# Norm factors on Pool instead of ACT and DVE, later xT transposes, and output-weight casts placed further back in the queues

## The chip, the cores and the metric

The kernel runs on one Trainium2 chip, on 8 cores, each with one of the 8 batch elements; the cores don't exchange data. A core has TensorE (PE), VectorE (DVE), ScalarE (ACT), GpSimd (Pool), and SyncE (SP), which issues most of the loads. The metric is device time in microseconds of the slowest core.

## What is computed

T = 2048 rows of D = 1024 per core. After a first layer norm, the block adds the state-space branch (with a layer norm of its own) and a feed-forward branch with ternary weights:

```python
xn = _layernorm(x, axis=-1)
x = x + _L0_attn_ref(xn, ...) + _L0_ffn_ref(xn, ...)

# _L0_attn_ref(x, ...): residual = x, second layer norm, then
dA = jnp.exp(-jnp.exp(log_A) * dt[:, None]); dB = B_param * dt[:, None]
h = dA * h + dB * u[..., None]                        # scan over time
y = jnp.einsum('dn,bdn->bd', C_param, h) + D_param * u
return residual + jnp.einsum('btd,ed->bte', y, W_out) + b_out

# _L0_ffn_ref(x, ...):
scale = jnp.maximum(jnp.mean(jnp.abs(w)), 1e-08)
w_t = jnp.clip(jnp.round(w / scale), -1.0, 1.0)       # W1 and W2
h = jax.nn.gelu(jnp.einsum('bsd,fd->bsf', x, w_t1) + b1, approximate=False)
return jnp.einsum('bsf,df->bsd', h, w_t2) + b2
```

## The kernel before

The program has one hand-written instruction order for each engine, with semaphores between them; no scheduler moves anything. What stands in a queue runs in that order.

**Stage 1, the state-space branch**, goes over 16 chunks c of 128 rows. For each chunk: `load_x` brings x into one of four buffers `gx`; DVE takes mean and variance (`stats`, `aggregate`, for groups of one chunk up to chunk 3 and of two chunks from chunk 4); the inverse root of the variance `rstd` and the shift `sb` give the normalised `xn` (`normalise`, on ACT, for chunk 0 on DVE); the second norm needs one more factor, `rstd2`, which scales the tables PP and cQ (`scale_PP` on ACT for chunks 1 to 3, `scale_tables` on DVE). DVE makes five products u = xn * gm (`make_u`, L854) and the running state S with its operand V (`make_V`, L870 and L874). PE then runs, for each chunk, `chunk_Q` (L1010, the chunk's part of the state), `ssm_local` (L1037, 40 matmuls into pY, within the chunk), `ssm_state` (L1044, what comes from earlier chunks), `transpose_V` (L1020), `transpose_x` (L1001, xn into the layout xT that stage 2 needs) and `wout` (L1061, 16 matmuls of 512 columns with the output weights). ACT evicts each: `yT_evict`, `VT_evict`, `xT_evict`, `yW_evict`; the last goes to memory through a Pool DMA (`store_yw`). The output weights come as four fp32 blocks (`load_wo` on SP) and are cast to bf16, two on ACT, two on DVE (`cast_wo`, L525 and L777); `wout(0)` waits for all four.

**The inverse roots before.** For a group, ACT takes the square root of the variance (`sqrt1`, L531), DVE the reciprocal, sb, and the second norm's variance y2 (`finish1`, L757 to L767), ACT its root (`sqrt2`, L537), DVE the reciprocal (`finish2`, L772). So each group passes from DVE to ACT and back twice. The constant EAGER = 12 shifts these, `normalise`, `wout` and the transposes between two orders, one for early chunks and one for late ones.

**At the start** PE and DVE also make six moments from the parameters (`power`, `moment`, L1080 and L1084, `moment_columns`, L1094), which `state_factors` on DVE (L827 to L835) turns into the factors that the state's operands need. `keep_clock` are matmuls without use.

**Beside stage 1** ACT sums |W1| over 16 blocks (`abs1`), which SP streams through buffers in the order W1_ORDER. After the last sum DVE sets the threshold and begins to quantise W1 (`quant`). **Stage 2** is the feed-forward part on PE: `mm1` (L1191, 4 x 32 tiles), then `mm2` (L1210); the last `wout(15)` stands ahead of it in PE's queue.

Pool's queue holds the x loads from chunk 4 on (each waits for the `normalise` that frees the buffer) and the `store_yw`s.

Of the kernel before, what the change touches and what calls it, by code (L numbers as in the profile page):

```python
# [45 lines left out]
EAGER = 12  # L46
# [52 lines left out]
def build_nc():  # L99
# [122 lines left out]
    sd = small("sd", M)  # L222
# [3 lines left out]
    sd2 = small("sd2", M)  # L226
# [40 lines left out]
    with st:  # L267
# [43 lines left out]
        s_sq1 = sem("s_sq1")  # L311
# [3 lines left out]
        s_sq2 = sem("s_sq2")  # L315
# [25 lines left out]
        with nc.Block() as blk:  # L341
            @blk.sync
            def _(sy):
# [36 lines left out]
                load_wo(0)  # L380
                load_wo(1)
                load_wo(2)
                load_x(2)
# [83 lines left out]
            def _(gp):  # L467
                gp.memset(Va[0][:, :], 0.0)
# [5 lines left out]
                gp.dma_start(wv[1][RW:RW + NV, :], cWE_in.ap()).then_inc(d_we, 16)  # L474
                def load_x(c):
# [19 lines left out]
                store_yw(3)  # L495
                for i in range(4, M):
                    if i + 7 < M:
                        load_x(i + 7)
                    store_yw(i)

            @blk.scalar
            def _(ac):
# [11 lines left out]
                ac.activation(dump[:, 1:2], cst[:, 0:1], AF.Sqrt, bias=cst[:, 2:3])  # L514
                mv3 = mv.ap().rearrange("p (c two) -> p c two", two=2)
# [11 lines left out]

                def sqrt1(g):
                    cs = slice(GROUPS[g][0], GROUPS[g][-1] + 1)
                    ac.wait_ge(s_var, g + 1)  # L530
                    ac.activation(sd.ap().unsqueeze(2)[:, cs, :], mv3[:, cs, 1:2], AF.Sqrt,  # L531
                                  bias=cst[:, 2:3]).then_inc(s_sq1, 1)

                def sqrt2(g):
                    cs = slice(GROUPS[g][0], GROUPS[g][-1] + 1)
                    ac.wait_ge(s_rs, g + 1)
                    ac.activation(sd2[:, cs], y2[:, cs], AF.Sqrt,  # L537
                                  bias=cst[:, 2:3]).then_inc(s_sq2, 1)
# [67 lines left out]
                gm_evict(0)  # L606
                sqrt1(0)
                gm_evict(1)
# [664 lines left out]
```

## Time and profile before

| | |
|---|---|
| times of 3 runs | 608.58, 610.12, 629.5 us (median 610.12) |
| profiled execution | 607.71 us, span of the slowest core 606.1 us (cores 600.9 to 606.1) |
| PE busy | 579.3 us, 96% |
| PE weight loads busy | 296.4 us, 49% |
| DVE busy | 271.5 us, 45% |
| ACT busy | 239.4 us, 40% |
| Pool busy | 21.6 us, 4% |
| read / written | 88.95 / 16.78 MB |

The profile is of one execution, on the core that was slowest. Busy time counts what an engine executes; overlapping matmuls are pipelined, so PE's share is not its share of peak. In the rows below "[x <-A y Lz]" means that the engine was idle for x us before the instruction and that the end of y on engine A (line z) released it.

### The profile page before, as it was taken

What the parts mean: (1) busy time and instruction counts of PE and PEld (TensorE: products, weight loads), DVE (VectorE), ACT (ScalarE), POOL (GpSimd) and SP (SyncE); (2) the same over time, 40 slices, a digit from 0 to 9 for tenths busy, and PEclk for the clock granted to TensorE, in tenths of its full rate; (3) what the DMA queues carried; (4) which work ended last, traced back from release to release, by engine and by line L of the source; (5) the groups of instructions that cost most, each with busy time, mean ns of one, the idle gap of its engine ahead of it and who ended that gap; (6) DMA issues with size and microseconds to landing.
All of it is one profiled execution on the core that took longest, in us unless ns stands there. A gap on an engine that the chain in (4) does not pass through costs nothing.

```text
span 606.1 us, 9213 instructions; the slowest of 8 cores (600.9 to 606.1 us)
## 1 busy us (share of the span) xinstructions
PE 579.3 (96%) x3478; PEld 296.4 (49%) x3478; DVE 271.5 (45%) x461; ACT 239.4 (40%) x310; POOL 21.6 (4%) x38
## 2 busy tenths in 40 slices
PE   7679799899999999999999999999999999999998
PEld 2456566567444444444444444444444444444445
DVE  6586978765699700000098861022332222222232
ACT  3677898788644577777344433100000000000000
POOL 3001111000100000000000000000000000000000
PEclk9779999899999999999999999999999999999999
DMA  6996768839778355571109952022333332232221
GB/s 161 325 335 256 252 213 317 301 124 356 247 269 278 151 202 198 201 258 47 45 31 304 317 197 83 1 105 104 111 134 135 135 113 104 105 105 104 105 104 70
DMA packets 21855, 106.10 MB, mean 175 GB/s; under 512 B 2922, under 2 KB 3434, under 8 KB 14388
## 3 DMA queue, kind: packets, MB, share of 16 engines
q1 hardware_dynamic: 17284, 90.50, 43.2%
q0 software_dynamic: 4128, 14.91, 7.0%
q8 instruction: 29, 0.48, 0.4%
q14 instruction: 14, 0.11, 0.1%
q10 hardware_dynamic: 400, 0.10, 0.1%
HBM read 88.95 MB, written 16.78 MB: 174 GB/s over the span
## 4 chain that ended last, share of the span: by engine, by line
PE 81%; DVE 6%; DMA 4%; ACT 3%; issue 3%; DVEq 2%; SPq 1%; ACTq 0%
PE pQ L1210 10%; PE pQ L1191 9%; PE pY L1210 9%; PE pX L1191 9%; PE pW L1210 9%; PE pW L1191 9%; PE pY L1191 9%; PE pX L1210 9%; PE pW L1061 5%; DMA wos<-wo 3%; DVE u L854 2%; PE pY L1037 2%; DVE bns L741 1%; DMA lBC_s<-abc 1%; DVEq L751 1%
## 5 line engine op out<-in xcount | busy, mean ns | idle before, releaser
L1210 PE MATMUL pQ<-w2q,h 128*128 128x512 fp8e4 (+1 forms) x288 | 59.6, 367 | 0.0
L1191 PE MATMUL pQ<-xT,w1q 128*128 128x512 bf16 x256 | 57.9, 379 | 0.6 <-DVE w1q L931 0.6
L1191 PE MATMUL pY<-xT,w1q 128*128 128x512 bf16 x256 | 57.9, 379 | 0.0
L1191 PE MATMUL pX<-xT,w1q 128*128 128x512 bf16 x256 | 57.9, 379 | 0.0
L1191 PE MATMUL pW<-xT,w1q 128*128 128x512 bf16 x256 | 57.9, 379 | 0.0
L1061 PE MATMUL pW<-woT,yT 128*128 128x512 bf16 x240 | 55.2, 383 | 1.8 <-ACT yws L603 1.8
L1210 PE MATMUL pY<-w2q,h 128*128 128x512 fp8e4 x256 | 55.9, 379 | 0.0
L1210 PE MATMUL pW<-w2q,h 128*128 128x512 fp8e4 x256 | 55.9, 379 | 0.0
L1210 PE MATMUL pX<-w2q,h 128*128 128x512 fp8e4 (+1 forms) x256 | 52.5, 366 | 0.0
L854 DVE TENSOR_TENSOR u<-xn,gm 128x1024 bf16<-128x1024 bf16 x80 | 49.5, 683 | 0.3 <-ACT gm L520 0.2
L1210 PEld LDWEIGHTS pQ<-w2q,h 128*128 128x128 bf16 x288 | 28.2, 98 | 30.5
L1191 PEld LDWEIGHTS pQ<-xT,w1q 128*128 128x128 fp8e4 x256 | 25.0, 98 | 31.0 <-issue 1.1
L1210 PEld LDWEIGHTS pY<-w2q,h 128*128 128x128 bf16 x256 | 25.1, 98 | 30.2
L1191 PEld LDWEIGHTS pX<-xT,w1q 128*128 128x128 fp8e4 x256 | 25.1, 98 | 30.2
L1191 PEld LDWEIGHTS pW<-xT,w1q 128*128 128x128 fp8e4 x256 | 25.0, 98 | 30.2
L1191 PEld LDWEIGHTS pY<-xT,w1q 128*128 128x128 fp8e4 x256 | 25.0, 98 | 30.2
L1210 PEld LDWEIGHTS pW<-w2q,h 128*128 128x128 bf16 x256 | 24.9, 97 | 30.3
L1037 PE MATMUL pY<-PP,u 128*128 128x128 bf16 x600 | 37.9, 224 | 0.7 <-ACT yT L596 0.7
L1210 PEld LDWEIGHTS pX<-w2q,h 128*128 128x128 bf16 x256 | 25.1, 98 | 27.0
L1061 PEld LDWEIGHTS pW<-woT,yT 128*128 128x128 bf16 x240 | 23.1, 99 | 27.5 <-issue 3.2
L1037 PEld LDWEIGHTS pY<-PP,u 128*128 128x128 bf16 x600 | 35.5, 101 | 1.3 <-issue 0.7
L950 DVE TENSOR_REDUCE tot<-ab 128x1 f32<-128x16 f32 x1 | 0.2, 171 | 76.5 <-ACT junk L707 76.5
(145 smaller groups left out, 610.9 us busy)
## 6 DMA issues: line engine op xcount, KB each, us to landing
kr<-w SPq DMA_DIRECT2D x20, 1024.0 KB, 6.2
p<-w SPq DMA_DIRECT2D x13, 1024.0 KB, 7.1
g<-w SPq DMA_DIRECT2D x9, 1024.0 KB, 9.3
scr_yw<-yws POOLq DMA_DIRECT2D x16, 512.0 KB, 7.0
xr<-x SPq DMA_DIRECT2D x16, 512.0 KB, 4.7
yr<-scr_yw SPq DMA_DIRECT2D x16, 512.0 KB, 5.5
out<-osb SPq DMA_DIRECT2D x15, 512.0 KB, 3.0
gx<-x POOLq DMA_DIRECT2D x12, 512.0 KB, 8.1
```

Of the source, the lines that this page charges most:

```text
L741: dv.bn_stats(bns[:, c * 12 + 6:c * 12 + 12], gx[c % 4][:, 512:1024])
L751: dv.drain()
L854: return dv.tensor_tensor(u[c % 2][k][:, :], xn[c % 4][:, :], gm[k][:, :], ALU.mult)
L950: dv.tensor_reduce(tot[:, 1:2], ab2[:, :], AX.X, ALU.add).then_inc(s_tot2, 1)
L1037: te.matmul(pS[c][:, bs], u[c % 2][k][:, bs], PP[c % 2][:, k * 128:(k + 1) * 128], start=(n == 0 and b % 4 == 0), stop=False)
L1061: inst = te.matmul(pO[i][:, hf * 512:(hf + 1) * 512], yT[i % 2][:, b * 128:(b + 1) * 128], woT[:, q:q + 512], start=(b == 0), stop=(b == 7))
L1191: inst = te.matmul(pA[n % 8], w1q8[:, f * 1024 + k * 128:f * 1024 + (k + 1) * 128], x3[:, k, :, :], start=(k == 0), stop=(k == 7))
L1210: inst = te.matmul(out_psum(e, n, cs), h[b][:, f * BT + tk * 128:f * BT + (tk + 1) * 128], w2q8[:, f * 1024 + cs.start:f * 1024 + cs.stop] ...
```

## The change

1. `finish` on Pool makes everything that `sqrt1`, `finish1`, `sqrt2` and `finish2` made: the variance plus EPS to the power -0.5 with Pool's pow, sb, sa, and the same for the second norm. Nine small operations for a group, with drains between those that depend on each other. ACT has no square root any more (and no table for it), DVE no reciprocal.
2. `transpose_x(c + 2)` and `xT_evict(c + 2)` in the loop over the chunks become (c + 1), behind `transpose_V` and `VT_evict`. The constant EAGER goes: one order for all chunks from 4 on, in which `wout(c - 1)` ends the chunk on PE and `normalise(c + 2)` ends it on ACT.
3. DVE's two weight casts stand behind `make_V(2)` (before: one ahead of `state_factors`, one behind `make_V(1)`), ACT's first one behind `scale_PP(1)`. x(2) is loaded ahead of the second weight block; its statistics stand ahead of `state_factors`.
4. `moment(4)` runs behind `transpose_x(0)`, with eight `keep_clock` matmuls in its old place; `keep_clock` writes pQ instead of pX.

```diff
-EAGER = 12
@@ SP
                 load_x(1)
                 load_wo(0)
+                load_x(2)
                 load_wo(1)
                 load_wo(2)
-                load_x(2)
                 load_wo(3)
@@ Pool
+                def finish(g):
+                    gp.wait_ge(s_var, g + 1)
...
+                    n = len(GROUPS[g])
+                    gp.tensor_scalar(v1, var, EPS, None, ALU.add)
+                    gp.drain()
+                    gp.tensor_tensor(rstd[:, cs], vt1[:, cs], nhalf[:, 0:n], ALU.pow)
+                    gp.drain()
+                    gp.tensor_tensor(sb.ap().unsqueeze(2)[:, cs, :], mean, r, ALU.mult)
+                    gp.tensor_tensor(v1, var, r, ALU.mult)
+                    gp.drain()
+                    gp.tensor_scalar(sb[:, cs], sb[:, cs], -1.0, None, ALU.mult)
+                    gp.drain().then_inc(s_rs, 1)
+                    gp.tensor_tensor(y2[:, cs], vt1[:, cs], rstd[:, cs], ALU.mult)
+                    gp.tensor_scalar(sa[:, cs], rstd[:, cs], 1.0, None, ALU.add)
+                    gp.drain()
+                    gp.tensor_scalar(y2[:, cs], y2[:, cs], EPS, None, ALU.add)
+                    gp.drain()
+                    gp.tensor_tensor(rstd2[:, cs], y2[:, cs], nhalf[:, 0:n], ALU.pow)
+                    gp.drain().then_inc(s_rs2, 1)
+
+                finish(0)
+                finish(1)
                 load_x(4)
                 load_x(5)
+                finish(2)
                 load_x(6)
                 store_yw(0)
+                finish(3)
                 load_x(7)
                 store_yw(1)
+                finish(4)
                 load_x(8)
                 store_yw(2)
                 load_x(9)
+                store_yw(3)
+                finish(GROUP_OF[6])
                 load_x(10)
...
+                for c in range(5, M + 1):
+                    store_yw(c - 1)
+                    if c + 6 < M:
+                        load_x(c + 6)
+                    if c % 2 == 1 and c + 3 < M:
+                        finish(GROUP_OF[c + 3])
@@ ACT, the loop after
+                for c in range(4, M):
                     yT_evict(c)
                     if c + 1 < M:
                         VT_evict(c + 1)
+                        xT_evict(c + 1)
+                    if c == 4:
+                        abs1(2)
+                    if c < M - 1:
+                        abs1(c - 1)
+                    if c >= M - 2:
+                        abs1(c)
+                    yW_evict(c - 1)
+                    if c + 2 < M:
+                        normalise(c + 2)
@@ DVE
                 stats_group(1)
-                finish1(1)
-                cast_wo(2)
+                stats(2)
                 state_factors()
                 make_u(1)
                 make_V(1)
+                dv.drain()
+                aggregate(2)
+                make_V(2)
+                cast_wo(2)
                 cast_wo(3)
-                stats_group(2)
-                make_V(2)
-                finish1(2)
+                make_u(2)
                 stats_group(3)
...
@@ PE
                 bc_pair(pB[4], 3)
-                moment(4)
+                keep_clock(8)
                 ssm_local(0)
...
                 transpose_x(0)
+                moment(4)
                 moment(5)
...
+                for c in range(4, M):
                     if c + 1 < M:
                         chunk_Q(c)
                     ssm_local(c)
                     ssm_state(c)
-                    if c + 3 < EAGER:
-                        wout(c - 1)
-                    if c + 2 < M:
-                        transpose_x(c + 2)
                     if c + 1 < M:
                         transpose_V(c + 1)
-                    if EAGER <= c + 3:
-                        wout(c - 1)
+                        transpose_x(c + 1)
+                    wout(c - 1)
```

**DVE's queue between the statistics of chunk 1 and its products.** Before (out<-in: what is written, then what is read; woT are the cast output weights, wos the fp32 blocks, Va and mst what `state_factors` writes, rstd_155 the second norm's factor):

```order
L745 BN_AGGR mv<-bns 128x2
L757 RECIPROCAL rstd<-sd 128x1 [waits s_sq1]
L759 TENSOR_TENSOR vt_152<-mv,rstd 128x1
L761 SCALAR_TENSOR_TENSOR sb<-mv,rstd 128x1
L765 TENSOR_TENSOR y_153<-vt_152,rstd 128x1
L767 TENSOR_SCALAR sa<-rstd 128x1
L777 CAST woT<-wos_59 128x2048 [waits d_wo2]
L827 TENSOR_TENSOR Va_99<-pQ,pars 128x8x6 [waits s_mom,d_par,s_zero]
```

The same place after:

```order
L727 BN_AGGR mv<-bns 128x2
L722 BN_STATS bns<-gx_107 128x6 [waits d_x2]
L723 BN_STATS bns<-gx_107 128x6
L787 TENSOR_TENSOR Va_99<-pQ,pars 128x8x6 [waits s_mom,d_par,s_zero]
L791 TENSOR_TENSOR Va_99<-pars 128x8
L787 TENSOR_TENSOR Va_100<-pQ,pars 128x8x6
```

The factors of chunk 1's norm and the cast, with its wait for the third weight block, are no longer ahead of `state_factors`; the statistics of chunk 2 are.

**Pool's queue around chunks 4 to 7, after** (before, only its DMA rows stood there; `scr_yw<-yws` is a `store_yw`, `gx<-x` a `load_x`, the rows between are one `finish`, here that of chunks 6 and 7):

```order
L501 DMA gx_106<-x 128x1024 [waits s_xn]
L506 DMA scr_yw<-yws_110 128x1024 [waits s_yWev]
L482 TENSOR_SCALAR vt_151<-mv 128x2 [waits s_var]
L484 TENSOR_TENSOR rstd<-vt_151,nhalf 128x2
L486 TENSOR_TENSOR sb<-mv,rstd 128x2
L487 TENSOR_TENSOR vt_151<-mv,rstd 128x2
L489 TENSOR_SCALAR sb<-sb 128x2
L491 TENSOR_TENSOR y_152<-vt_151,rstd 128x2
L492 TENSOR_SCALAR sa<-rstd 128x2
L494 TENSOR_SCALAR y_152<-y_152 128x2
L496 TENSOR_TENSOR rstd_154<-y_152,nhalf 128x2
L501 DMA gx_107<-x 128x1024 [waits s_xn]
```

The nine operations stand behind a store that waits for ACT's `yW_evict(3)`, and a load of x stands behind them.

**ACT's queue around `normalise(6)`.** Before (rw and res are blocks of W1 for `abs1`; xn_87 is the buffer of chunk 6):

```order
L531 ACTIVATE sd<-mv,cst 128x2 [waits s_var]
L596 ACTIVATE yT_89<-pY 128x1024 [waits s_ssm,s_wout]
L545 ACTIVATE xn_87<-gx_107,sb,rstd 128x1024 [waits s_rs,s_Q,s_u]
L537 ACTIVATE sd_154<-y_153,cst 128x2 [waits s_rs]
L589 ACTIVATE rwA,ab_159<-rwA 128x2048 [waits d_rw0]
L603 ACTIVATE yws_110<-pW 128x1024 [waits s_wout,d_yw1]
```

After:

```order
L614 ACTIVATE yT_89<-pY 128x1024 [waits s_ssm,s_wout]
L589 ACTIVATE VTs_98<-pQ 128x512 [waits s_vtr,s_ssm]
L582 ACTIVATE xT<-pX 128x1024 [waits s_T]
L607 ACTIVATE rwA,ab_158<-rwA 128x2048 [waits d_rw0]
L607 ACTIVATE junk,ab_158<-res_0_50 128x2048 [waits d_res1_0,s_ab1]
L621 ACTIVATE yws_110<-pW 128x1024 [waits s_wout,d_yw1]
L563 ACTIVATE xn_87<-gx_107,sb,rstd 128x1024 [waits s_rs,s_Q,s_u]
L614 ACTIVATE yT_90<-pY 128x1024 [waits s_ssm,s_wout]
```

`normalise(6)` came right behind yT(4); it now comes behind two |W1| sums and yW(3), and the square roots are gone.

## Rows read from the trace of the kernel before

**Rows 1.** By stage: window, length; busy PE, PEld, DVE, ACT, POOL; clock; DMA share, GB/s.
```profile
33.20:62.40 29.20, 24.36 (x275) 17.95 (x273) 21.44 (x59) 22.63 (x30) 2.79 (x5) 0.94 0.78 277
62.40:114.50 52.10, 45.59 (x519) 32.09 (x516) 40.71 (x105) 45.93 (x57) 6.91 (x13) 0.97 0.83 286
114.50:143.80 29.30, 28.19 (x343) 20.48 (x340) 20.63 (x49) 24.61 (x28) 2.13 (x4) 1.00 0.58 194
...
161.10:606.10 445.00, 442.26 (x2080) 203.43 (x2080) 160.00 (x164) 118.25 (x162) 1.25 (x1) 1.00 0.41 144
```
**Rows 2.** Timeline (start, length, instruction): `ssm_local` of chunks 1, 3, 4, 6, 10.
```profile
33.22 4.04 PE L1037 MATMUL pY<-PP,u 128*128 128x128 bf16 x40
...
53.64 2.39 PE L1037 MATMUL pY<-PP,u 128*128 128x128 bf16 x40 [0.68 <-ACT yT L596]
...
62.41 2.68 PE L1037 MATMUL pY<-PP,u 128*128 128x128 bf16 x40
...
80.07 2.39 PE L1037 MATMUL pY<-PP,u 128*128 128x128 bf16 x40
...
114.48 2.39 PE L1037 MATMUL pY<-PP,u 128*128 128x128 bf16 x40
```
**Rows 3.** Timeline, PE: a `wout`, then `ssm_local` of chunks 12 and 13.
```profile
126.12 3.61 PE L1061 MATMUL pW<-woT,yT 128*128 128x512 bf16 x16
...
129.77 2.39 PE L1037 MATMUL pY<-PP,u 128*128 128x128 bf16 x40
...
136.78 2.39 PE L1037 MATMUL pY<-PP,u 128*128 128x128 bf16 x40
```
**Rows 4.** Timeline: moments on PE, casts and `state_factors` on DVE.
```profile
23.73 1.07 PE L1084 MATMUL pQ<-wk,cCs 128*64 128x512 f32 x2
...
25.97 1.03 PE L1094 MATMUL pQ<-cEs,mrow 64*128 64x12 f32 x8 [1.17 <-ACT mrow L619]
...
29.67 1.23 DVE L777 CAST woT<-wos 128x2048 bf16<-128x2048 f32 x1 [3.70 <-DMA wos<-wo]
30.82 0.22 DVE L827 TENSOR_TENSOR Va<-pQ,pars 128x48 bf16<-128x48 f32 x1
...
35.83 1.22 DVE L777 CAST woT<-wos 128x2048 bf16<-128x2048 f32 x1
```
**Rows 5.** Timeline: chunk 0 from its variance to xn and PP.
```profile
14.32 0.21 DVE L745 BATCH_NORM_AGGREGATE mv<-bns 128x2 f32<-128x12 f32 x1
...
16.28 0.81 DVE L812 TENSOR_SCALAR xn<-gx,rstd,sb 128x1024 bf16<-128x1024 f32 x1
...
18.25 0.55 DVE L848 TENSOR_SCALAR PP<-PF,rstd 128x640 bf16<-128x640 f32 x1 [0.23 <-issue]
```
**Rows 6.** Timeline, Pool: a one-column memset and a DMA issue.
```profile
0.49 0.10 POOL L100 MEMSET const-float32-0.0<- 128x1 f32 x1 [0.49 <-issue]
...
46.02 0.54 POOL L482 DMA_DIRECT2D scr_yw<-yws  x1 [2.44 <-ACT yws L603]
```
**Rows 7.** Timeline, ACT: one late chunk.
```profile
132.76 1.02 ACT L596 ACTIVATE yT<-pY 128x1024 bf16<-128x1024 f32 x1 [1.63 <-PE pY L1044]
...
133.69 1.02 ACT L564 ACTIVATE xT<-pX 128x1024 bf16<-128x1024 bf16 x1
...
134.59 0.60 ACT L571 ACTIVATE VTs<-pQ 128x512 bf16<-128x512 bf16 x1
...
135.07 1.25 ACT L545 ACTIVATE xn<-gx,sb,rstd 128x1024 bf16<-128x1024 f32 x1
136.20 1.92 ACT L589 ACTIVATE junk<-kr 128x2048 bf16<-128x2048 f32 x1
...
138.09 1.03 ACT L603 ACTIVATE yws<-pW 128x1024 f32<-128x1024 f32 x1
```
**Rows 8.** Waits: who waited for whom, us in total, times, longest.
```profile
DVE rstd L757 <- ACT sd L531: 12.1, 8, 3.4
```
**Rows 9.** Timeline, PE: the first matmuls of the feed-forward part.
```profile
161.12 3.61 PE L1191 MATMUL pQ<-xT,w1q 128*128 128x512 bf16 x16 [0.59 <-DVE w1q L931]
```

More of the change, by code:

```diff
@@ L225, in build_nc @@
     y2 = small("y2", M)
-    sd2 = small("sd2", M)
+    nhalf = small("nhalf", 2)
     rstd2 = small("rstd2", M)
@@ L467, in _ @@
             def _(gp):
+                gp.memset(nhalf[:, :], -0.5)
                 gp.memset(Va[0][:, :], 0.0)
@@ L809, in _ @@
                 power(4)
-                finish1(0)
-                dv.drain()
+                dv.wait_ge(s_rs, 1)
                 dv.tensor_scalar(xn[0][:, :], gx[0][:, :], rstd[:, 0:1], sb[:, 0:1],
@@ L841, in scale_tables @@
                 def scale_tables(c):
-                    if c == GROUPS[GROUP_OF[c]][0]:
-                        finish2(GROUP_OF[c])
+                    dv.wait_ge(s_rs2, GROUP_OF[c] + 1)
                     if c == 0:
@@ L900, in _ @@
                 stats_group(4)
-                finish1(4)
                 for c in range(3, M):
-                    if c % 2 == 0 and c + 2 < EAGER:
-                        finish1(GROUP_OF[c + 2])
-                    if c % 2 == 1 and EAGER <= c + 3 < M:
-                        finish1(GROUP_OF[c + 3])
                     if c + 1 < M:
@@ L909, in _ @@
                         make_u(c + 1)
-                    if c % 2 == 1 and c + 3 < EAGER:
+                    if c == 4:
+                        stats_group(GROUP_OF[6])
+                    if c >= 5 and c % 2 == 1 and c + 3 < M:
                         stats_group(GROUP_OF[c + 3])
-                    if c % 2 == 0 and EAGER <= c + 4 < M:
-                        stats_group(GROUP_OF[c + 4])
                 def set_threshold(src, o):
@@ L1099, in keep_clock @@
                     for _ in range(n):
[L1100 removed]
+                        te.matmul(pQ[:, 0:128], Va[0][:, 0:128], Va[0][:, 0:128],
                                   start=True, stop=True)
@@ L1133, in _ @@
                 ssm_state(1)
-                wout(0)
                 transpose_V(2)
                 transpose_x(2)
+                wout(0)
+                chunk_Q(2)
                 wout(1)
-                chunk_Q(2)
                 ssm_local(2)
                 ssm_state(2)
+                transpose_V(3)
                 transpose_x(3)
-                transpose_V(3)
                 chunk_Q(3)
@@ L1146, in _ @@
                 wout(2)
+                transpose_V(4)
                 transpose_x(4)
-                transpose_V(4)
-                chunk_Q(4)
-                ssm_local(4)
-                ssm_state(4)
-                wout(3)
-                transpose_x(5)
-                transpose_x(6)
-                transpose_V(5)
-                for c in range(5, M):
+                for c in range(4, M):
                     if c + 1 < M:
```

113 lines of the change are left out of this document (15 added, 98 removed).

## The prediction, as put on record before the run

> **What bounds the kernel now.** I read the table by stage first [rows 1]. From 161.1 us to the end (the two products of the feed-forward part) PE is busy 442.3 of 445.0 us at a granted clock of 1.00, and no edit touches an instruction there. What can move is the stage ahead of it: when the first L1191 matmul starts, 161.12 us [rows 9]. In that stage the same table shows PE busy 28.2 of 29.3 us late (chunks 10 to 13), but only 24.4 of 29.2 and 45.6 of 52.1 us in the two stretches before: 4.8 and 6.5 us of idle.
>
> The starts of `ssm_local` turn this into a pace [rows 2, 3]. From chunk 12 to chunk 13 a chunk takes 136.78 - 129.77 = 7.0 us, full of PE work; its longest piece, `wout`, is half of it (3.61 us, some 3.5 from its start to the next piece's). From chunk 4 (62.41) to chunk 10 (114.48) six chunks take 52.07 us, 8.7 each, where six at the late pace would take 42.0. Both stretches hold six `wout`s, so 10 us are lost there. Chunk 1 starts at 33.22 and chunk 3 at 53.64.
>
> The waits name two causes. DVE waits 12.1 us in eight pieces for ACT's small square roots [rows 8], in order, with its tables, products and state updates queued behind. And at 29.67 DVE's queue had stood 3.70 us for the third output weight to land, with `state_factors` behind that cast, so at 30.82 [rows 4]. Its input, the moment columns, was done at 25.97 + 1.03 = 27.0.
>
> **The change part by part.** Times are of the profiled execution: span 606.1 us, 607.71 us by the clock of the runs, against a median of 610.12 over three runs of which the lowest is 608.58. I take 607.7.
>
> 1. **Casts moved, x(2) loaded earlier.** DVE's wait for the weight goes. `state_factors` then waits for the moments, which come later: `moment(4)` now runs behind `ssm_local(0)`, so the columns end one warm fp32 product (1.07 us, [rows 4]) later, 28.1. Gain 30.8 - 28.1 = 2.7 us. The eight `keep_clock` matmuls put in its old place lie in a gap in which PE waits for PP of chunk 0; I cost them at nothing, and without that cover at under 1 us. What is late next is `wout(0)`, which needs all four casts: the fourth weight is used by DVE at 35.83 before, the cast takes 1.2 us (as in [rows 4]), so 37.0, while PE reaches `wout(0)` at 37.3 through ACT's queue. That leaves 2.6 us of gain.
>
> 2. **Inverse roots on Pool.** Per group 9 small operations on one or two columns, 5 of them (with four drains) before s_rs, 4 before s_rs2. Before, the same for chunk 0 ran from the variance (14.32 + 0.21) to xn at 16.28, and to PP at 18.25 [rows 5]: 1.75 and 3.7 us. No Pool arithmetic is in the trace. Nearest rows below: a one-column memset, 0.10 us; nine make 0.9 us. Above: a Pool DMA issue, 0.54 us [rows 6]; nine make 4.9 us. A drained step needs read, write and drain, and pow is more than an add, so I take 0.39 us a step: P1 = 2.0 to s_rs, P2 = 1.5 more to s_rs2. For chunk 0 that is 3.5 against 3.7 us, so no gain or loss at the start. From DVE it removes the 12.1 us of waits and seven small operations a group; from ACT 18 square roots of 0.3 us and a table load.
>
> 3. **Pool's queue.** Pool also issues the x loads and the yW stores, in order. `finish(3)` stands behind `store_yw(0)` and `finish(5)` behind `store_yw(3)`; each issue waits for ACT's eviction and takes 0.54 us [rows 6]. I walked the queues with the durations of [rows 7] (yT and xT 0.9, VT 0.5, xn 1.1, abs 1.9, yW 1.0 us from start to start).
>  Chunk 3: its variance is there at about 41.9; the store is issued by 42.5; s_rs2 at 42.5 + 3.5 = 46.0; then on ACT PP 0.8, yW(1) 1.0, abs 1.9 + 0.2, yT(2) 0.9: `ssm_local(3)` at 50.8 instead of 53.64, gain 2.8.
>  Chunk 4: state of chunk 3 at 53.8, `wout(2)` 3.5, transposes and chunk_Q 1.2: 58.4 instead of 62.41, gain 4.0. Chunk 5 follows at the full pace, 65.4.
>  Chunk 6: ACT ends xn(5) at 61.4, then yT 0.9, VT 0.5, xT 0.9, two abs 3.8 and yW(3) 1.0: 68.6. The store 0.5, P1 2.0, xn(6) 1.2: 72.4, where PE wanted it at 68.7. Transpose 0.5, `wout(4)` 3.5 and chunk_Q 0.3 follow: 76.7 instead of 80.07, gain 3.4.
>
> 4. **Transposes one chunk later, no EAGER switch.** From chunk 6 on nothing is late: ACT needs 0.9 + 0.5 + 0.9 + 1.9 + 1.0 + 1.1 = 6.4 us per chunk, DVE 20.63 of 29.3 us [rows 1] less what is removed, Pool's results are due 5 us after they come. So 7.0 us a chunk: chunk 10 at 104.7 instead of 114.48, gain 9.8. One more hitch goes: chunks 10 to 12 took 129.77 - 114.48 = 15.3 us where two at the late pace take 14.0, so 11.1 from chunk 12 on. At the end ACT is the queue that decides when the last |W1| sum is ready; it now has xT(15) in the last stretch, 0.9 us [rows 7]. Gain 10.2 us.
>
> Sum: 2.7 - 0.1 (wout(0)) + 0.2 (chunk 3) + 1.2 (chunk 4) - 0.6 (chunk 6) + 6.4 (to chunk 10) + 1.3 - 0.9 = 10.2. 607.7 - 10.2 = **597.5 us**.
>
> The Pool price enters three times: chunk 0 once P1 + P2 passes 3.7, chunk 3 with P1 + P2, chunk 6 with P1. With 0.9 us in all chunk 3 is held by yW(1) instead (1.2 us better) and chunk 6 is 1.5 better: gain 12.9, 594.8 us. With 4.9 us: 1.2 + 1.4 + 0.7 lost, gain 6.9, 600.8 us.
>
> **The rivals.**
> - *DVE and Pool stand in each other's way.* [rows 1] speaks against much of it: late DVE is busy 70%. For it: Pool's nine steps fall into the same stretch as the five products. If each Pool step waits out half a product (0.3 us) and stops DVE for 0.2 us, P1 + P2 becomes 6.2 us: that costs chunk 0 2.5, chunk 3 2.7 and chunk 6 1.4 us less what lies beside idle DVE time (most of chunk 0), some 5 us. Gain about 5: 602.7 us. The Trainium skill, page "SBUF — State Buffer", section "Who interferes with whom", says that a DVE instruction with two SBUF inputs and a Pool instruction that reads SBUF exclude each other for a whole instruction; no row here shows it, since Pool reads nothing before.
> - *Pool is slow the first time.* A first arithmetic operation on Pool that costs several microseconds would hold xn(0), and everything behind. With 6 us (taken as eleven of Pool's 0.54 us issues) less 0.2 of slack: gain 4.4, 603.3 us. The Trainium skill's "GPSIMD Engine Reference", section 2.1, gives approximately 6 us for the first call of a freshly loaded kernel; whether the plain operations count as that the page doesn't say. No row shows such a gap ahead of Pool's first memset.
> - *Slower than before: the Pool chain itself.* If a drained Pool step with pow costs 0.9 us, P1 = 4.5 and P2 = 3.6. Chunk 0 loses 8.1 - 3.7 = 4.4, chunk 3 8.1 - 3.5 = 4.6, chunk 6 4.5 - 2.0 = 2.5 us against my sum: 11.5, so 609.0 us. The point from which it decides, where 23 steps less 9.2 eat the 10.2, is a step of 0.84 us. Against it: no Pool row of small size exceeds 0.54 us.
> - *The gain is given back to loads.* The stage needs the same bytes in 10 us less. DMA share is 0.83 in the middle and 0.58 late [rows 1], so there is room; the x loads are issued later on Pool, and if one lands 1 us late in each of three groups, it costs 3 us: 600.5 us. Inside my range.
>
> **How the numbers follow.** My forecast (gain 6.9 to 12.9) has 0.60, the collision 0.15, the first-time cost or a chain of 0.6 to 0.8 us a step 0.15, slower than before 0.07, and 0.03 for a gain over 13. The likeliest one's own range is 594.8 to 600.8. Leaving out no more than 2 in 10 I give 592.5 to 606.0, which takes in the collision and the slow first call. Two per cent is about what a measurement of this kernel tells from no change: 12.2 us, so below about 596. That needs a step under some 0.2 us or a smoother walk than mine: 0.30. Within 2%: 0.65. Slower by over 2% needs a step of well over a microsecond: 0.05.
>
> **What would show it.** In the profile after: s_var to xn(0) about 2.0 us and to PP(0) 3.5 us, the small Pool rows 0.1 to 0.5 us; `state_factors` at 28.1 with no wait for a weight; chunk 3 near 50.8, chunk 4 near 58.4, PE waiting about 3.5 us for xn(6) behind `store_yw(3)`, chunk 6 near 76.7; chunks 7 to 14 each 7.0 us; the first L1191 matmul (other line number) at 151 us, and 445 us from there. I am wrong if the late pace isn't 7.0, if Pool's steps cost 0.6 us or more, or if DVE's products get longer than 0.68 us beside Pool's work. A granted clock that is low for longer around 20 to 28 us would delay the moments by up to 1 us.

## The result, and the profile after

The changed kernel takes 645.98 us (median of four runs, 644.96 to 647.02). The ratio to the kernel before is 1.060, 95% interval 1.056 to 1.064: 6% slower, where 597.5 us and a gain were forecast. (The runs of before beside it are 608.58 and 610.12 us; two more, 627.84 and 629.5, show a lower clock on one die, and such runs are left out of every ratio here, though not of the medians.) In the profiled execution the slowest core, 7, has a span of 645.4 us, the others 632.0 and more.

The page of the changed kernel first: busy time, then the granted clock in 40 slices of 16 us.

```profile
span 645.4 us, 9264 instructions; the slowest of 8 cores (632.0 to 645.4 us)
## 1 busy us (share of the span) xinstructions
PE 586.7 (91%) x3486; PEld 300.6 (47%) x3486; DVE 264.7 (41%) x401; ACT 234.6 (36%) x288; POOL 51.5 (8%) x129
...
PEclk9779778998799999999999999999999999999999
```

The digit is 7 or 8 in seven of the first 11 slices and 9 in all later ones. The table by stage (window, length; busy PE, PEld, DVE, ACT, POOL; clock; DMA share, GB/s) answers to [rows 1]:

```profile
30.70:57.30 26.60, 15.42 (x121) 9.93 (x122) 11.29 (x22) 10.76 (x12) 3.97 (x12) 0.75 0.73 249
...
65.70:138.60 72.90, 54.59 (x587) 39.18 (x588) 39.00 (x86) 47.14 (x52) 19.17 (x49) 0.87 0.68 202
138.60:146.40 7.80, 7.17 (x90) 5.12 (x87) 6.62 (x15) 6.57 (x7) 1.45 (x3) 1.00 0.96 346
164.70:182.20 17.50, 9.49 (x91) 5.99 (x88) 4.37 (x9) 6.71 (x9) 3.25 (x9) 0.71 0.56 198
200.00:645.00 445.00, 442.27 (x2080) 203.45 (x2080) 160.52 (x165) 118.75 (x162) 1.25 (x1) 1.00 0.42 144
```

The feed-forward part is what it was: 442.27 busy of 445.00 us at full clock. All the loss lies ahead of it. It begins at 200.43 us instead of 161.12 [rows 9]. The rows show the pattern that begins with chunk 4: one chunk of each pair takes 7 to 8 us (138.6 to 146.4, chunk 10), the other 8.8 to 21 (164.7 to 182.2, chunk 13, with no engine busy for more than 9.5 of its 17.5 us).

The waits say for whom (engine, line, for whom; us in total, times, longest):

```profile
POOL rstd L484 <- issue: 50.5, 9, 12.2
ACT xn L563 <- POOLq L490: 41.9, 7, 11.0
DVE PP L807 <- POOLq L497: 38.4, 6, 12.6
PE pX L954 <- ACT xn L563: 36.7, 8, 11.8
```

Read from below: PE waits 36.7 us for xn, ACT makes xn late because it waits 41.9 us for the end of Pool's first half, and inside Pool's chain 50.5 us stand ahead of one instruction, the first pow (L484), "issue": the profile shows nothing that it waits for. (Of the nine pieces one, of chunk 0, is 0.33 us; eight make 50.1.) In the code there is one thing between L482 and L484: a drain.

Pool's timeline shows the same chain twice, for the groups of chunk 1 and of chunk 2 (start, length, instruction, idle before):

```profile
25.14 0.22 POOL L482 TENSOR_SCALAR vt<-mv 128x1 f32<-128x1 f32 x1 [6.35 <-DVE mv L727]
25.51 0.57 POOL L484 TENSOR_TENSOR rstd<-vt,nhalf 128x1 f32<-128x1 f32 x1
...
29.27 1.23 POOL L501 DMA_DIRECT2D gx<-x  x2 [0.70 <-ACT xn L563]
34.10 0.22 POOL L482 TENSOR_SCALAR vt<-mv 128x1 f32<-128x1 f32 x1 [3.60 <-DVE mv L727]
43.03 0.57 POOL L484 TENSOR_TENSOR rstd<-vt,nhalf 128x1 f32<-128x1 f32 x1 [8.71 <-issue]
...
159.38 0.53 POOL L506 DMA_DIRECT2D scr_yw<-yws  x1 [6.14 <-ACT yws L621]
159.94 0.24 POOL L482 TENSOR_SCALAR vt<-mv 128x2 f32<-128x2 f32 x1
172.41 0.72 POOL L484 TENSOR_TENSOR rstd<-vt,nhalf 128x2 f32<-128x2 f32 x1 [12.23 <-issue]
```

For chunk 1 the step over the drain takes 25.51 - 25.14 = 0.37 us, as I had costed it (0.39). For chunk 2, with two x loads issued at 29.27 to 30.5, it takes 8.9 us. The last group, behind the store of 159.38, takes 12.5. The DMA view gives, from issue to landing, of the stores issued at 54.28 and at 159.38:

```profile
scr_yw<-yws POOLq DMA_DIRECT2D x1, 512.0 KB, 3.1
...
scr_yw<-yws POOLq DMA_DIRECT2D x1, 512.0 KB, 12.8
```

54.28 + 3.1 = 57.4, and that group's pow starts at 57.58; 159.38 + 12.8 = 172.2, pow at 172.41. The load issued at 107.09 (5.3 us) has landed by 112.4, pow at 112.66; that of 122.92 (8.0 us) by 130.9, pow at 131.19. In all eight groups behind the first load the pow starts 0.2 to 0.3 us after the last landing; the two groups ahead of it have gaps of 0.33 us and none. The other seven cores show the same: over all eight there are 59 gaps of 0.9 us and more, and each ends 0.2 to 0.43 us after the last landing of a transfer that Pool had issued. That is the theory: **a drain on Pool waits until the transfers that Pool issued have landed**, though here nobody needs them.

The end of the chain, on PE, in the last pair:

```profile
164.68 2.39 PE L990 MATMUL pY<-PP,u 128*128 128x128 bf16 x40
...
175.75 1.01 PE L954 MATMUL pX<-cIDb,xn 128*128 128x128 bf16 x8 [8.01 <-ACT xn L563]
176.56 5.58 PE L1014 MATMUL pW<-woT,yT 128*128 128x512 bf16 x16
...
185.53 3.62 PE L1014 MATMUL pW<-woT,yT 128*128 128x512 bf16 x16
```

After 8.01 us of waiting the next `wout` takes 5.58 us, the following one 3.62: over 164.7 to 182.2 the granted clock is 0.71, parts of it at 1.2 GHz, parts at 2.4. Here the wait cost PE 2 us beyond its own length.

### The profile page after: what moved, and what is told of

It reads as the page before. It is cut to its first block, busy times and chain, and to the rows that moved or that the text cites. A ratio compares the mean times of both kernels' runs of the same rounds, so it can differ in the third digit from the quotient of the medians.

```text
span 645.4 us, 9264 instructions; the slowest of 8 cores (632.0 to 645.4 us)
## 1 busy us (share of the span) xinstructions
PE 586.7 (91%) x3486; PEld 300.6 (47%) x3486; DVE 264.7 (41%) x401; ACT 234.6 (36%) x288; POOL 51.5 (8%) x129
## 4 chain that ended last, share of the span: by engine, by line
PE 79%; issue 11%; ACT 5%; POOLq 2%; DVE 1%; POOL 1%; DVEq 0%; DMA 0%; ACTq 0%
PE pQ L1153 9%; PE pQ L1134 9%; PE pY L1134 9%; PE pW L1153 9%; PE pY L1153 9%; PE pX L1134 9%; PE pW L1134 9%; PE pX L1153 8%; PE pW L1014 5%; ACT xn L563 2%; PE pY L990 1%; PE pX L954 1%; POOLq L485 1%; ACT yws L621 1%; PE pQ L1033 1%
## 5 line engine op out<-in xcount | busy, mean ns | idle before, releaser
L1014 PE MATMUL pW<-woT,yT 128*128 128x512 bf16 x240 | 61.4, 414 | 1.9 <-ACT yws L621 1.9
L954 PE MATMUL pX<-cIDb,xn 128*128 128x128 bf16 x128 | 10.9, 235 | 36.7 <-ACT xn L563 36.7
L990 PE MATMUL pY<-PP,u 128*128 128x128 bf16 x600 | 39.6, 229 | 3.9 <-ACT yT L614 3.5
L1153 PEld LDWEIGHTS pQ<-w2q,h 128*128 128x128 bf16 x288 | 28.2, 98 | 30.5
L1014 PEld LDWEIGHTS pW<-woT,yT 128*128 128x128 bf16 x240 | 24.9, 106 | 32.1 <-issue 11.3
L990 PEld LDWEIGHTS pY<-PP,u 128*128 128x128 bf16 x600 | 37.2, 103 | 4.8 <-issue 4.1
```

What stands on the lines that cost most here:

```text
L954: inst = te.transpose(xbank[c % 2][:, b * 128:(b + 1) * 128], xn[c % 4][:, b * 128:(b + 1) * 128], cID[:, :])
L990: te.matmul(pS[c][:, bs], u[c % 2][k][:, bs], PP[c % 2][:, k * 128:(k + 1) * 128], start=(n == 0 and b % 4 == 0), stop=False)
L1014: inst = te.matmul(pO[i][:, hf * 512:(hf + 1) * 512], yT[i % 2][:, b * 128:(b + 1) * 128], woT[:, q:q + 512], start=(b == 0), stop=(b == 7))
L1153: inst = te.matmul(out_psum(e, n, cs), h[b][:, f * BT + tk * 128:f * BT + (tk + 1) * 128], w2q8[:, f * 1024 + cs.start:f * 1024 + cs.stop] ...
```

## The experiments

The rivals: the pow itself is slow in those places, or DVE and Pool stand in each other's way (both then independent of transfers), or the new order, not the roots, makes the gaps.

**Semaphores for the drains.** In `finish` each of the seven drains (the expectation says eight) goes. Five become a semaphore, raised by the operations ahead and waited for by Pool; behind the two that raised s_rs and s_rs2 the last operation now raises them itself:

```diff
-                    gp.tensor_scalar(v1, var, EPS, None, ALU.add)
-                    gp.drain()
+                    step(gp.tensor_scalar(v1, var, EPS, None, ALU.add))
+                    settled()                    # gp.wait_ge(s_fin, count)
```

> The changed kernel with each of Pool's eight drains per group replaced by a wait on a semaphore that the operation itself raises; order and DMAs as in the changed kernel. Theory D (a drain on Pool also waits until the DMAs that Pool issued before it have landed: the gaps of 8.7, 2.5, 7.8, 4.5, 7.3, 6.2 and 12.2 us ahead of the first pow of a group end 0.2 us after a landing): those gaps fall to 0.2 to 0.4 us, the first matmul of the feed-forward part starts at 150 to 153 us instead of 200, time 597 to 600 us. Theory Q (Pool completes nothing behind an own DMA until that has landed, drain or not): gaps and time stay, 640 to 648 us. Theory P (Pool is kept off SBUF by DVE's operations with two SBUF inputs): gaps stay where DVE is busy, 625 to 648 us.

Measured: 608.15 us, ratio to before 0.997 (0.994 to 1.000). Pool's timeline:

```profile
130.96 0.53 POOL L516 DMA_DIRECT2D scr_yw<-yws  x1 [6.44 <-ACT yws L631]
131.52 0.37 POOL L492 TENSOR_SCALAR vt<-mv 128x2 f32<-128x2 f32 x1
132.04 0.87 POOL L494 TENSOR_TENSOR rstd<-vt,nhalf 128x2 f32<-128x2 f32 x1
```

The store of 130.96 takes 11.8 us to land, and the pow (now L494) starts 1.1 us after the issue. No gap stands ahead of this pow on any core, and the 38 us are gone with nothing else changed. The gaps went as theory D had it; the time is 8 us above its 597 to 600. The section on the prediction takes up why. The times of this version fall into two groups, four runs of 603.7 to 605.0 us and five of 608.0 to 610.9. In the profiled run seven cores have spans of 600.1 to 602.8 us and one, core 5, has 606.7: rows of this run are of that core unless another is named.

**Drains kept, transfers issued by ACT.** The x loads and the yW stores move from Pool's queue to ACT's:

```diff
-                def load_x(c):                   # on Pool
-                    gp.wait_ge(s_xn, c - 3)
-                    gp.dma_start(gx[c % 4][:, :],
+                def load_x(c):                   # on ACT, store_yw too
+                    ac.wait_ge(s_xn, c - 3)
+                    ac.dma_start(gx[c % 4][:, :],
```

> The changed kernel with all drains kept, but the x loads from chunk 4 on and the stores of yW issued by ACT instead of Pool, each one operation behind the one it depends on. Pool then has only arithmetic. Theory D and theory Q: no gap over 0.4 us ahead of pow; ACT pays 28 DMA issues with short waits, so 597 to 606 us. Theory P: the gaps stay, because DVE does the same work; 625 to 648 us.

Measured: 608.26 us, 0.999 (0.997 to 1.000). Pool's timeline in chunk 2, drains in place:

```profile
35.64 0.22 POOL L482 TENSOR_SCALAR vt<-mv 128x1 f32<-128x1 f32 x1 [6.62 <-DVE mv L718]
36.00 0.57 POOL L484 TENSOR_TENSOR rstd<-vt,nhalf 128x1 f32<-128x1 f32 x1
36.71 0.19 POOL L486 TENSOR_TENSOR sb<-mv,rstd 128x1 f32<-128x1 f32 x1
36.85 1.17 POOL L487 TENSOR_TENSOR vt<-mv,rstd 128x1 f32<-128x1 f32 x1
```

0.36 us from the first operation to the pow, and 0.36 to 0.38 in every later group of this run. A drain alone costs next to nothing, and so does a transfer alone; it takes both on Pool. One thing more changed with the issuer: the profile lists the transfers under "q0 software_dynamic" in the changed kernel and under "q10 hardware_dynamic" here, so the run doesn't tell whether Pool's own issue or that kind of queue is what a drain waits for. The time, like that of the first version, is above the 597 to 606 us of theory D.

**Pairs of probes in the kernel before.** Pool makes two additions on a scratch column with a drain between them behind `store_yw` 5, 9 and 13, and with a semaphore between them behind `store_yw` 7, 11 and 14:

```diff
+                def probe_drain():
+                    gp.tensor_scalar(pr[:, 2:3], pr[:, 0:1], 1.0, None, ALU.add)
+                    gp.drain()
+                    gp.tensor_scalar(pr[:, 4:5], pr[:, 2:3], 1.0, None, ALU.add)
```

> The kernel before with probes on Pool that nobody waits for: two one-column additions with a drain between them (once with no DMA of Pool in flight, and behind the stores of chunks 5, 9 and 13) and two with a semaphore wait between them (once at the start, and behind the stores of chunks 7, 11 and 14). Theory D: from the first to the second addition 0.3 to 0.5 us with no DMA in flight; behind a store the drain pair is 3 to 12 us apart and ends 0.2 us after the store has landed, the semaphore pair 0.3 to 0.5 us apart. Theory Q: both pairs behind stores 3 to 12 us apart. Theory P: both short. Time as before, 607 to 612 us, since the x loads are issued well ahead.

Measured: 615.23 us, with a span of 613.6 (the other of its two runs took 686.6 us). Pool's timeline:

```profile
86.87 0.54 POOL L485 DMA_DIRECT2D scr_yw<-yws  x1 [2.46 <-ACT yws L628]
87.43 0.53 POOL L489 TENSOR_SCALAR pr<-pr 128x1 f32<-128x1 f32 x1
98.17 2.29 POOL L491 TENSOR_SCALAR pr<-pr 128x1 f32<-128x1 f32 x1 [10.21 <-ACT xn L570]
...
102.03 0.54 POOL L485 DMA_DIRECT2D scr_yw<-yws  x1
102.59 0.22 POOL L497 TENSOR_SCALAR pr<-pr 128x1 f32<-128x1 f32 x1
102.97 0.21 POOL L500 TENSOR_SCALAR pr<-pr 128x1 f32<-128x1 f32 x1 [0.15 <-POOL pr L497]
```

The store of 86.87 takes 10.5 us to land, at 97.4; the second addition of the drained pair starts at 98.17. (The profile's releaser, ACT's xn, is only what else happened then.) The store of 102.03 takes 16.5 us, and the pair with the semaphore is done in 0.6; the pair behind the store of 147.13, which lands after 11.6 us, has its second addition at 149.77. In the other two drained pairs behind a store the second addition starts at 135.18 with a landing at 134.8, and at 168.08 with one at 167.8. So it is the drain, in another kernel and with other operations, whatever the pow does. The time is 3 us above the 607 to 612 that was expected; x loads stand behind the drained pairs too (the one behind 98.17 is issued at 100.40), which may be why.

The second addition at 98.17 also lasts 2.29 us instead of 0.21. DVE at that time:

```profile
97.30 3.09 DVE L879 TENSOR_TENSOR u<-xn,gm 128x1024 bf16<-128x1024 bf16 x5
```

It ends with the last product, at 100.4. The Trainium skill ("SBUF — State Buffer", "Who interferes with whom") has that a DVE instruction with two SBUF inputs excludes a Pool instruction that reads SBUF; these 2.29 us agree, with the addition that here a read waited out the rest of a back-to-back series.

**Only the first drain replaced.** In the changed kernel the drain between L482 and L484 alone becomes a semaphore:

```diff
-                    gp.tensor_scalar(v1, var, EPS, None, ALU.add)
-                    gp.drain()
+                    gp.tensor_scalar(v1, var, EPS, None, ALU.add).then_inc(s_fin, 1)
+                    gp.wait_ge(s_fin, g + 1)
```

> The changed kernel with only the first drain of each group replaced by a semaphore that the instruction ahead raises. Theory A (any drain of Pool waits until the transfers that Pool issued have landed): the idle time of 2.5 to 12.2 us moves one instruction on, from ahead of the first power to behind it, with the same end (issue plus landing), and the span stays at 640 to 648. Theory B (the first instruction pair of a group is slow for another cause, the switch from issuing to computing or the first use of the power): the gap is gone or stays ahead of the power, and in the first case the span falls to about 607.

Measured: 637.61 us in a single run. Pool's timeline for the last group, whose store was issued at 152.59 and took 11.9 us to land, at 164.5:

```profile
153.15 0.24 POOL L483 TENSOR_SCALAR vt<-mv 128x2 f32<-128x2 f32 x1
153.53 1.00 POOL L485 TENSOR_TENSOR rstd<-vt,nhalf 128x2 f32<-128x2 f32 x1
164.75 0.20 POOL L487 TENSOR_TENSOR sb<-mv,rstd 128x2 f32<-128x2 f32 x1 [10.22 <-issue]
```

The pow starts at once and the gap stands behind it, 39.9 us in nine pieces over the run. It moved to the next drain, as theory A had it. On all eight cores there are 56 such gaps, each over 0.17 to 0.35 us after the last landing. The span, 636.1 us, is 4 us under the range of theory A, with gaps of 39.9 us in all against 50.5. How long they are depends on how long the transfers take, and that differs between cores and runs: core 0 of the changed kernel has gaps of 39.1 us and a span of 632.0. Why this run had shorter ones wasn't followed up.

**Roots ahead of the stores.** Back to what the change could do. With semaphores, `finish(3)` is put ahead of `store_yw(0)` and `finish(5)` ahead of `store_yw(3)`:

```diff
+                finish(3)
                 store_yw(0)
-                finish(3)
...
+                finish(GROUP_OF[6])
                 store_yw(3)
-                finish(GROUP_OF[6])
```

> As the first kernel of this set (semaphores for drains), and the factors of chunk 3 stand ahead of the store of chunk 0, those of chunks 6 and 7 ahead of the store of chunk 3. Under theory D and the walk of the prediction (chunk 3 waits 0.5 us, chunk 6 about 1.2 us for a store's place in the queue) it is 1 to 2 us faster than the first kernel; if those places don't matter, the same within 0.5 us. Under theory Q 636 to 646 us.

Measured: 603.25 us, 0.991 (0.988 to 0.993). Chunk 3's `ssm_local` starts at 53.20 where it started at 58.23 with semaphores alone, but hardly any of these 5 us is the work of the new order: on the other seven cores of the run with semaphores alone chunk 3 starts at 51.9 to 54.0, and here on all eight at 52.0 to 53.5. What the order changes is chunk 6, which follows chunk 5 after 10.3 to 12.1 us on the eight cores, where it was 13.2 to 13.7. The median span of the cores goes from 602.4 to 599.6 us. So about 3 us come from the order. The rest of the 5 us between the two kernels' times fits a slowest core without the mishap of core 5, which the experiment with chunk 2's variance shows; no run separates it.

**The casts alone, the roots alone.** Two versions of the kernel before. In one only the weight casts move (DVE's two behind `make_V(2)`, ACT's first behind `scale_PP(1)`). In the other only the roots go to Pool, with semaphores; every order of before stays.

```diff
                 finish1(1)
-                cast_wo(2)
                 state_factors()
                 make_u(1)
                 make_V(1)
-                cast_wo(3)
                 stats_group(2)
                 make_V(2)
                 finish1(2)
+                cast_wo(2)
+                cast_wo(3)
```

> The kernel before with only the output weights' casts moved (VectorE's two behind the moments of chunk 2, ScalarE's first behind the scaled table of chunk 1); roots and order of TensorE as before. Theory A (step 1 of the prediction: the cast ahead of the state factors costs 2.7 us on the path): state factors at about 28.1 in place of 30.8, chunk 1 at about 31, total 606 to 608, ratio 0.995 to 0.998. Theory B (what is gained at chunk 1 is lost again at the first output product, which waits for the casts): chunk 2 as before at 42 or later, total 608 to 612.

> The kernel before in its own order of TensorE, ScalarE and VectorE (transposes for xT where they were, casts where they were), only the roots made by Pool, with semaphores between Pool's instructions and no drain; no square roots on ScalarE, no reciprocals on VectorE. Theory A (the gain of the semaphore versions, 0.99 to 0.997, is from the order): total 606 to 610, ratio 0.997 to 1.003. Theory B (it is from the roots, 0.3 to 8 us waits of ScalarE and VectorE for each other that are gone, 12.1 us of VectorE's in all): total 600 to 605, ratio 0.985 to 0.994. Theory C (the roots by Pool arrive later than before in that order, behind loads and stores that wait): above 612.

Measured: casts alone 608.32 us, 1.000 (0.998 to 1.001); roots alone 610.13 us, 1.002 (1.001 to 1.004). The casts' version is theory B. PE's timeline, its chunk 1 and chunk 4, and the start of the feed-forward part:

```profile
29.59 4.43 PE L1037 MATMUL pY<-PP,u 128*128 128x128 bf16 x40
...
61.57 2.68 PE L1037 MATMUL pY<-PP,u 128*128 128x128 bf16 x40
...
161.48 3.61 PE L1191 MATMUL pQ<-xT,w1q 128*128 128x512 bf16 x16 [0.59 <-DVE w1q L931]
```

Chunk 1 is 3.6 us earlier than in [rows 2] (`state_factors` at 27.17 against 30.82), chunk 4 0.8 us, and the feed-forward part begins at 161.48 against 161.12. So 2.8 us of what the head of the stage gains are lost again by chunk 4, and the rest by chunk 10 (114.71 against 114.48). The roots' version falls to theory A: waits of DVE for ACT's square roots are gone (12.1 us before [rows 8]), but that order gives nothing for it.

**Chunk 2's variance earlier.** On the version with the roots ahead of the stores, DVE aggregates chunk 2 ahead of `state_factors`:

```diff
                 stats(2)
+                dv.drain()
+                aggregate(2)
                 state_factors()
                 make_u(1)
                 make_V(1)
-                dv.drain()
-                aggregate(2)
```

> As the run with semaphores and the Pool order (603.25 us, 0.9906 of before), and one thing more: VectorE aggregates the moments of chunk 2 directly behind its statistics, ahead of the state factors, so Pool makes roots for chunk 2 at about 30 us and not at 36.5 to 38.9 beneath VectorE's casts of the output weights. Theory A (the casts hold Pool: 1.28 and 1.17 us on instructions that last 0.1 to 0.7 elsewhere, and the wait of TensorE that follows, 2.83 us, leaves it at the lower clock for the output product behind it, 6.0 us in place of 3.5): xn(2) starts by 37.5 in place of 39.4, no wait of ScalarE for Pool there, chunk 2's local products at about 44 in place of 47.2, total 599 to 601, ratio 0.984 to 0.987. Theory B (chunk 2 is late for the order of ScalarE and TensorE, not for Pool): chunk 2 stays within 1 us of 47.2 and the total at 602.5 to 604.

Measured: 602.77 us, 0.991 (0.989 to 0.992); no different from its base, so theory B. My premise was off. In the run with semaphores alone DVE's casts had held Pool on core 5 (its L496 and L497, 1.28 and 1.17 us) and PE had gone on late and at the lower clock, a granted 0.60 over the 6 us of `wout(0)`:

```profile
36.49 1.28 POOL L496 TENSOR_TENSOR sb<-mv,rstd 128x1 f32<-128x1 f32 x1
37.73 1.17 POOL L497 TENSOR_TENSOR vt<-mv,rstd 128x1 f32<-128x1 f32 x1
...
40.89 1.01 PE L964 MATMUL pX<-cIDb,xn 128*128 128x128 bf16 x8 [2.83 <-ACT xn L573]
41.70 6.01 PE L1024 MATMUL pW<-woT,yT 128*128 128x512 bf16 x16
```

In the base version's profile the roots came 1 us earlier and had their first half done before the casts began at 36.44; xn(2) was not late there, and `wout(0)` took 3.62 us. The other seven cores of the run with semaphores alone say the same: there the casts fell on Pool's second half, for which xn doesn't wait, `transpose_x(2)` waited 0.4 us, and `wout(0)` started at 37.8 to 39.9 at the full clock. The collision is on every core, but whether it falls on the half that counts is a matter of a microsecond. With the early variance chunk 2 starts at 47.58, against 47.16.

**The group of chunks 6 and 7 earlier.** On top, its statistics stand ahead of `make_u(4)`, where DVE idled 3.59 us, and its roots directly behind `finish(4)`:

```diff
                         make_V(c + 1)
+                        if c == 3:
+                            stats_group(GROUP_OF[6])
                         make_u(c + 1)
...
                 finish(4)
+                finish(GROUP_OF[6])
                 load_x(8)
                 store_yw(2)
                 load_x(9)
-                finish(GROUP_OF[6])
```

> The run before plus the same for the group of chunks 6 and 7: its statistics stand ahead of the products of chunk 4, where VectorE idled 3.59 us, and its roots directly behind those of chunks 4 and 5 in Pool's queue. Theory A (the 12.1 us between the local products of chunks 5 and 6 come from roots that start at 70.5 and from the 2.53 us wait of TensorE with the lower clock after it): chunk 6 follows 7.0 to 8 us after chunk 5, the total is 594 to 597, ratio 0.976 to 0.981, and the kernel beats both. Theory B (another wait ends there, a store or the load of chunk 6 or 7 that lands at about 56 to 58): chunk 6 still follows more than 10 us after chunk 5 or chunk 4 is later by what was gained, total 599 to 601.

Measured: 603.23 us, 0.992 (0.990 to 0.994), no gain, and neither theory as written: chunk 6 follows chunk 5 after 8.4 us, near what theory A had, but the time is above both ranges. Chunk 6 is on time, chunk 7 isn't. PE, then DVE:

```profile
74.63 2.39 PE L1000 MATMUL pY<-PP,u 128*128 128x128 bf16 x40
...
80.56 0.38 PE L983 MATMUL pQ<-cIDb,Va 128*128 128x128 bf16 x4 [3.10 <-DVE Va L843]
...
86.58 2.39 PE L1000 MATMUL pY<-PP,u 128*128 128x128 bf16 x40
```
```profile
77.98 0.69 DVE L732 BATCH_NORM_STATS2 bns<-gx 128x6 f32<-128x512 f32 x1 [2.60 <-DMA gx<-x]
```

The statistics of chunk 9 wait for its load, which took 14.9 us from issue to landing with DMA engines busy to 0.92 between 40 and 80 us; behind them in DVE's queue stands `make_V(7)`, for which PE waits. 11.95 us between chunks 6 and 7, where it was 12.1 between 5 and 6 with the roots ahead of the stores and 13.2 in the base: the stall changed its place. That is core 7; on the other cores of this run it is 8.35 to 9.95 us.

**The waiting statistics behind the moments.** One line moves: the statistics of each later pair go between `make_V` and `make_u` of the chunk ahead of the pair.

```diff
                         if c == 3:
                             stats_group(GROUP_OF[6])
+                        if c >= 6 and c % 2 == 0 and c + 2 < M:
+                            stats_group(GROUP_OF[c + 2])
                         make_u(c + 1)
-                    if c >= 5 and c % 2 == 1 and c + 3 < M:
-                        stats_group(GROUP_OF[c + 3])
```

> The last version (groups of chunks 2 and of 6, 7 early; 603.23 us, 0.9919), with one move: the statistics of chunks 8 and 9 (and so of each later pair) stand between the moments and the products of the chunk ahead of the pair, where before they stood ahead of both; what waits for the load of chunk 9 (2.60 us of VectorE, 3.10 us of TensorE in the profile) is then no longer ahead of the moments of chunk 7, which TensorE waits for. Theory A (that wait and the lower clock after it are what is left of the stall that was moved from chunk 6 to chunk 7): chunk 7's local products follow chunk 6's after 7 to 8 us in place of 11.95, the FFN starts at 150 to 152 in place of 154.8, total 597 to 600. Theory B (the slowest core's time is no longer set in this stage by single waits, as the transfers fill the DMA engines to 0.92 between 40 and 80 us and will be late in another place): the stall appears at a later chunk, total 601 to 604.

Measured: 599.98 us, ratio 0.986 (0.984 to 0.987): the best version, 8.5 us under the kernel before. PE's `ssm_local` of chunks 6, 7, 8 and the start of the feed-forward part:

```profile
75.38 2.39 PE L1000 MATMUL pY<-PP,u 128*128 128x128 bf16 x40
...
83.72 2.39 PE L1000 MATMUL pY<-PP,u 128*128 128x128 bf16 x40
90.73 2.34 PE L1000 MATMUL pY<-PP,u 128*128 128x128 bf16 x39
...
152.75 3.61 PE L1144 MATMUL pQ<-xT,w1q 128*128 128x512 bf16 x16 [0.59 <-DVE w1q L894]
```

The load is still late (DVE waits 1.52 us for it), but what PE needs stands ahead of it; 8.3 us from chunk 6 to 7, then 7.0. The total is at the end of theory A's range; the step to chunk 7 and the start of the feed-forward part lie just beyond theirs. On four cores DVE doesn't wait for the load, chunk 7 follows after 7.0 us, and the spans are 593.0 to 594.0 us. On the other four it waits 0.9 to 1.6 us, PE loses 1.9 to 3.1 us between chunks 6 and 9, and the spans are 597.2 to 597.8 us. So the stall is smaller, not gone, and it still lies on the slowest core.

## Why the prediction was wrong, point by point

- **The step that failed** is in part 2, "I take 0.39 us a step", applied to every group. It is right for the operations (measured: 0.22, pow 0.57, 0.19, 0.24 us; the five of chunk 1 take 1.8 us, 2.1 with their last drain to the start of xn, against 2.0, and the rest 1.6 against 1.5), and for a drain with nothing in flight. It is wrong for a drain in a queue that also issues transfers. I read Pool's queue for what waits behind what, and took a DMA issue to be over after its 0.54 us; for the drain it is over at the landing, 12.8 us later in the last group. That is 50.5 us of Pool's time and 38 us of the total, in the comparison of the semaphore version with the changed kernel. By the page of each, PE's busy time grew by 6.1 us (586.7 against 580.6: the lower clock) and its idle time by the other 32.6 of the 38.7 us between the spans.
- **The slower rival had the right sign and the wrong mechanism.** It asked for drained steps of 0.84 us and more, with a chance of 0.07 (and 0.05 for slower by over 2%), since no small Pool row exceeded 0.54 us. The trace of before holds no drain on Pool, so it could not bound its cost; the bounds were drawn from operations. The question missed was what a drain waits for.
- **Part 1 (casts).** `state_factors` at 28.77 us (28.1 forecast): near. That it is worth 2.6 us of the total was wrong: alone the casts are worth nothing (1.000).
- **Part 3 (Pool's queue).** Even without the stall the walk was too fast. With semaphores chunks 3, 4, 5 and 6 start at 58.23, 65.39, 73.06 and 86.48, against 50.8, 58.4, 65.4 and 76.7. Of the 7.4 us at chunk 3, `wout(0)` starts at 41.70 in place of 37.3 and takes 2.5 us longer at the lower clock; the rest is yT(2) behind the roots that wait in Pool's queue for `store_yw(0)`, which comes at 49.39 and not at 42.5. At chunk 6 I had forecast PE's wait for xn as 3.5 us (it is 4.08) and left out the lower clock behind it (granted 0.74 from 81 to 87 us, where `wout(4)` takes 4.84 us and not 3.6). From chunk 5 to 6 it is 13.4 us against 11.3, so the loss of 0.6 us in my sum should have been 2.7.
- **Part 4 (7.0 us a chunk afterwards).** Right where nothing stalls: 86.48 to 114.89 for chunks 6 to 10 is 7.1 each. The tail is right as well: the feed-forward part runs 445 us. With semaphores it begins at 161.66, 10.7 late against 151, which is the delay of chunk 6 (9.8 us) carried on. So without the drains the forecast would still have been too low: 608.15 measured, 10.7 us above 597.5 and 2 above its range. Some 4 us of that are the mishap of one core. On the other seven chunk 3 starts at 51.9 to 54.0, chunk 6 at 80.0 to 82.4 and the feed-forward part at 155.0 to 157.8, and the four lower of the nine times, 603.7 to 605.0, lie inside the range. The walk followed one core, and the time is that of the slowest of eight.
- **Rival "collision".** It is there: 1.0 to 2.3 us on single Pool instructions beneath casts, up to 2.3 beneath a series of products, 0.6 to 0.7 beneath each single product. DVE's five products stay at 3.09 us beside it, so the 0.2 us that I had DVE lose a step isn't seen. For chunk 0 my forecast had no loss, the rival 2.5 us: in the changed kernel chunk 0 takes 2.6 us from its variance to xn and 5.75 to PP, against 2.0 and 3.5 forecast, with two of Pool's steps taking 0.7 us each, one beside DVE's xn and one beside a product. `ssm_local(0)` starts at 20.39 where it started at 19.13. No run isolates what that is worth in the total.
- **Rival "slow first call".** Not there: Pool's first operation starts 0.2 us after the end of chunk 0's variance (13.93 against 13.75) and takes 0.47 us, its first pow 0.58.
- **Rival "given back to loads".** It came true, but only once the rest was fast: x(9) holds DVE 2.6 us in the version with early groups.

Two counts in part 2 are off without changing the sum: a group had six small operations on DVE, not seven, and ACT had 20 square roots, not 18.

What stays open: the new order with the roots left on ACT and DVE wasn't run, so how the 1.4% of the best version divide between the order and the roots is known only in part (roots in the old order: nothing; roots and new order: 0.3%, which its interval doesn't tell from nothing, to 1.4%, by where they stand in the queues). Open, too, is whether a drain waits in this way on an engine other than Pool.

## What to carry to other kernels

Before moving small dependent operations to Pool while it also issues transfers, look at what separates them: here a drain waited for the transfers, a semaphore raised by the operation didn't. And when a trace lacks an operation, ask what it waits for, not only how long its neighbours take. A stall that PE meets in order is often only moved by an earlier start; it goes when what may be late (here the statistics that wait for a load) stands behind what PE needs next.

## What the runs showed of the hardware that was not expected

- What stands behind a drain on Pool starts 0.2 to 0.8 us after the landing of the transfers that Pool issued: eight groups of the changed kernel (gaps of 0.9 to 12.2 us), the same groups on its other cores, and three probes (2.8 to 10.7 us from start to start). With the same transfers issued by ACT it takes 0.36 us from the start of one operation to the next. With a semaphore it is 0.38 us, with a transfer of 16.5 us in flight.
- Pool's pow on 128 partitions takes 0.57 us for one column and 0.72 for two; additions and products 0.18 to 0.25, where DVE doesn't hold them.
- DVE's casts of 128x2048 fp32, with one input, held Pool's small reads for 1.2 to 1.3 us, about a cast's own length, and on another core of the same run one for 2.29 us, the length of both casts (2.36). The same section of the Trainium skill's "SBUF — State Buffer" counts casts among the instructions that can exclude Pool; these rows agree.
- After a wait of 2.83 us, with 1.33 us of another shortly before it, PE's granted clock was 0.60 and a `wout` of 3.6 us took 6.0; after a single wait of 1.08 us it was 1.00 and the `wout` took 3.61.
